# Eight PSUM banks dealt out anew: three for the scores, two for the row maxima

## What is computed

```python
x = x + 0.5 * ffn(layernorm(x), ...)        # 8 experts, top 2 for each row, a gate at the end
x = x + attention(layernorm(x), ...)        # 16 heads of 8 columns, causal, a linear bias by distance
x = x + 0.5 * ffn(layernorm(x), ...)

# attention, for each of 8 batch entries:
att = einsum("bhqd,bhkd->bhqk", q, k) / sqrt(8) + alibi      # 16 heads, 512 queries, 512 keys
att = softmax(where(causal, att, -inf), axis=-1)
y = einsum("bhqk,bhkd->bhqd", att, v)
out = y @ o_w + o_b
```

## Time and profile before

| | |
|---|---|
| time, median of 3 runs | 887.24 us (885.19 to 888.77) |
| profiled execution, its own time | 885.58 us |
| its span in the profile | 883.8 us |
| mean granted TensorE clock | 0.913 of full speed |
| TensorE matmul busy | 683.1 us (77%) |
| VectorE, ScalarE, GpSimd busy | 568.2, 410.8, 485.6 us |

### The profile page before, as it was taken

The page is one execution under the profiler, slowest core; times in us unless marked ns, Lnnn a source line. Parts: engine busy times, 40 slices in busy tenths (PEclk is TensorE's granted clock), DMA queues, the critical chain, the costliest instruction groups (busy, mean ns, idle before and its releaser), DMA issues.

```text
span 883.8 us, 16149 instructions
## 1 busy us (share of the span) xinstructions
PE 683.1 (77%) x4719; PEld 492.3 (56%) x4719; DVE 568.2 (64%) x1922; ACT 410.8 (46%) x931; POOL 485.6 (55%) x588
## 2 busy tenths in 40 slices
PE   1465667979897798997988979999997777838760
PEld 1355656979793354654646545455544466837750
DVE  3675545968767876876767767787673235745538
ACT  2243411545560265664545645556554655615530
POOL 2656554034512666576866768373645466566661
PEclk9968777988898899998999999999997999969985
DMA  8614544744348313023050240302201235233525
GB/s 242 205 48 117 132 123 115 183 112 105 94 113 192 110 31 98 18 65 87 2 130 21 49 103 1 98 17 55 61 13 53 85 78 167 75 93 84 175 96 154
DMA packets 89825, 84.04 MB, mean 95 GB/s; under 512 B 14561, under 2 KB 72556, under 8 KB 89580
## 3 DMA queue, kind: packets, MB, share of 16 engines
q1 hardware_dynamic: 74472, 57.51, 25.8%
q0 software_dynamic: 8800, 19.72, 7.5%
q10 hardware_dynamic: 6468, 5.79, 2.8%
HBM read 43.84 MB, written 31.13 MB: 85 GB/s over the span
## 4 chain that ended last, share of the span: by engine, by line
PE 46%; DVE 15%; another core or an unknown queue 11%; issue 7%; ACT 7%; SPq 5%; ACTq 3%; DMA 3%; POOL 1%; DVEq 0%; POOLq 0%
PE bank L2361 6%; PE bank L2271 6%; PE bank L2401 6%; PE bank L2286 6%; PE bank L2426 6%; SPq L595 4%; DVE mx_of L1923 3%; PE pair L2449 2%; PE bank L2363 2%; ACT beside_parts L1254 2%; DMA qT<-mT_zero 2%; PE pair L2213 2%; PE bank L2246 1%; ACT arena L1326 1%
## 5 line engine op out<-in xcount | busy, mean ns | idle before, releaser
L1326 ACT ACTIVATE arena<-bank 128x512 f32<-128x512 f32 x320 | 184.0, 599 | 175.2 <-PE bank L2401 147.1
L1923 DVE TENSOR_REDUCE mx_of<-bank 128x4 f32<-128x512 f32 x320 | 204.2, 684 | 81.9 <-PE bank L2361 42.9
L2401 PE MATMUL bank<-qT,kZ 128*128 128x512 f32 (+3 forms) x512 | 156.9, 377 | 19.2 <-ACT arena L1326 12.4
L975 POOL TENSOR_SCALAR_AFFINE_SELECT arena<-arena 128x256 f32<-128x256 f32 (+1 forms) x192 | 95.4, 521 | 123.9 <-ACT arena L1326 122.5
L2361 PE MATMUL bank<-kZ,qT 128*128 128x512 f32 x320 | 148.5, 481 | 15.7 <-DVE mx_of L1923 6.2
L2401 PEld LDWEIGHTS bank<-qT,kZ 128*128 128x128 f32 x512 | 95.7, 197 | 49.2 <-ACT arena L1326 24.1
L868 POOL DMA_INDIRECT z_rows<-beside_kZ,place x80 | 78.7, 984 | 51.5 <-DVE place L1685 29.8
L2361 PEld LDWEIGHTS bank<-kZ,qT 128*128 128x128 f32 x320 | 63.1, 200 | 70.7 <-issue 31.4
L885 POOL DMA_INDIRECT sums<-y_rows,y_place x56 | 54.4, 971 | 84.9 <-DMA y_rows<-arena 70.0
L2426 PE MATMUL bank<-arena,vA 128*9 128x512 f32 (+3 forms) x1024 | 92.4, 440 | 5.2 <-POOL arena L975 2.7
L1254 ACT ACTIVATE beside_parts<-bank,hidden_bias 128x128 f32<-128x128 f32 x160 | 45.5, 381 | 69.6 <-remote 44.0
(11 more groups left out here) (286 smaller groups left out, 1306.7 us busy)
## 6 DMA issues: line engine op xcount, KB each, us to landing
arena<-z_rows SPq DMA_DIRECT2D x128, 66.0 KB
qT<-parts SPq DMA_DIRECT2D x42, 128.0 KB
kZ<-parts SPq DMA_DIRECT2D x168, 32.0 KB
y_rows<-arena SPq DMA_DIRECT2D x20, 264.0 KB, 3.3
kZ<-bias_k_r SPq DMA_DIRECT2D x8, 512.0 KB
beside_kZ<-y_rows SPq DMA_DIRECT2D x7, 528.0 KB, 3.9
z_rows<-in_spare SPq DMA_DIRECT2D x4, 528.0 KB
z_rows<-in_spare SPq DMA_DIRECT2D x32, 66.0 KB
```

Source lines behind the costliest of these rows:

```text
L975: g_.affine_select(out=cut, in_=cut, compare_op=ALU.is_ge, fill=0.0, base=0, pattern=[[0, 2], [0, blocks], [1, P]], channel_multiplier=-1) ...
L1326: a_(dst, src, ACT.Exp).then_inc(exp_ok.sem, 1)
L1923: v.tensor_reduce(mx_of[:, queries, :, t, keys], ps_a[n % NA][:, :].rearrange("p (q n) -> p q n", q=NQ), AX.X, ALU.max).then_inc(reduced.s ...
L2401: return mm(outp, kZ[u][:, h, lo:lo + P], qT[u][:, t, lo:SEQ], start=start, stop=True, skip_group_check=(kind != "full"))
```

## The change

Bank 4 goes from the maximum units to the score units. `ps_a` has two banks (0, 1): maximum unit n waits for the reduction of unit n - 2. `ps_b` has three (2, 3, 4): score unit n waits for the exponential of unit n - 3. Since 40 is no multiple of three, the score ring doesn't start anew with each batch but runs on over its end: unit n of batch b is in bank (40 b + n) mod 3. The last batch has a ring of five (2, 3, 4, 0, 1), entered where the other one stopped; its first five units wait for all exponentials of the batch before and for all reductions. Three waits at the seam to the second experts are worked out anew from the banks (in the diff in this order: the first transposes into banks 2 and 3, the first `up` into 0 and 1, the first `down` into bank 4), and batch 0's first score units wait for `y_weighted` too, since bank 4 was one of the experts'.

```diff
-        ps_a, ps_b, ps_o, ps_m = [banks[0], banks[1], banks[4]], banks[2:4], banks[5], banks[6:8]
+        ps_a, ps_b, ps_o, ps_m = banks[0:2], banks[2:5], banks[5], banks[6:8]
         NA = len(ps_a)
-        ps_b_last = ps_b + ps_a[:2]
+        ps_b_last = ps_b + ps_a
+        last_first = N_UNITS * (BATCH - 1) % len(ps_b)
 
         def score_bank(b, n):
-            ring = ps_b_last if isinstance(b, int) and b == BATCH - 1 else ps_b
-            return ring[n % len(ring)], len(ring)
+            if b == BATCH - 1:
+                return ps_b_last[(n + last_first) % len(ps_b_last)], len(ps_b_last)
+            return ps_b[(N_UNITS * b + n) % len(ps_b)], len(ps_b)
+
+        def last_unit_in(bank_):
+            return max(n for n in range(N_UNITS) if score_bank(BATCH - 1, n)[0] is bank_)
...
-                        wait(pe, exp_ok, BATCH - 1, N_UNITS - 3 + q)
+                        wait(pe, exp_ok, BATCH - 1, 1 + last_unit_in(ps_x[q % 2]))
...
-                        wait(pe, exp_ok, BATCH - 1, N_UNITS - 1 + p)
+                        wait(pe, exp_ok, BATCH - 1, 1 + last_unit_in(ps_up[p % 2]))
...
-                        wait(pe, reduced, BATCH - 1)
+                        wait(pe, exp_ok, BATCH - 1)
...
                 if early(b, 0) and n < ring:
                     wait(pe, x_out, 0)
-                elif ring == 2:
-                    pe.wait_ge(exp_ok.sem, exp_ok.value(b, n - 1))
-                elif n < 2:
-                    wait(pe, exp_ok, b - 1)
+                    wait(pe, y_weighted, 0)
+                elif b < BATCH - 1:
+                    pe.wait_ge(exp_ok.sem, exp_ok.value(b, n - ring + 1))
                 elif n < ring:
+                    wait(pe, exp_ok, b - 1)
                     wait(pe, reduced, b)
                 else:
                     wait(pe, exp_ok, b, n - ring + 1)
```

More of the change, by code:

```diff
@@ L2388, in scores @@
                     wait(pe, x_out, 0)
-                elif ring == 2:
-                    pe.wait_ge(exp_ok.sem, exp_ok.value(b, n - 1))
-                elif n < 2:
+                    wait(pe, y_weighted, 0)
+                elif b < BATCH - 1:
+                    pe.wait_ge(exp_ok.sem, exp_ok.value(b, n - ring + 1))
+                elif n < ring:
                     wait(pe, exp_ok, b - 1)
-                elif n < ring:
                     wait(pe, reduced, b)
```

## The result

| | before | after |
|---|---|---|
| median of 4 runs each | 888.0 us (885.19 to 892.74) | 907.4 us (903.75 to 910.38) |
| profiled execution, span | 885.58, 883.8 us | 903.75, 901.9 us |
| mean granted TensorE clock | 0.913 | 0.907 |

The account below looks back on a forecast made before the run. TensorE was taken to bound batches 0 to 6, VectorE the maxima of batch 0. 16 (maximum bank) + 3 (maxima) - 2 (score bank) + 0.5 (seam) = +17.5 us on 885.58, as a median 905 us, range 888 to 922.

Parts of the forecast that it names:

- third maximum bank: Batches 0 to 6: its loss makes TensorE wait for later reductions, 2.3 us a batch, +16 us (+7 to +39).
- third score bank: Waits of score units for exponentials: only short ones, mostly in batch 0, go; -2 us (0 to -12.4).
- A: Slot 0, four maximum units in a row: unit 3 waits for the second reduction, not the first; +0.6 us a batch.
- maxima of batch 0: Stretch led by VectorE: two-bank loop slower, first half hidden by a DMA wait, second not; +3 us (1 to 5).
- C: Slot 11, two maximum units in a row: the second waits +0.8 us, half counted before the first `values`; +0.4 a batch.
- D: Slots 20 to 22, reductions run after layer norm statistics: units 26 and 27 wait one reduction longer; +0.65 us a batch.
- E: Slot 28, run of five reductions: maximum unit 33 waits longer; +0.35 us a batch.
- F: Slot 33: unit 39 waits +0.6 us longer, of which the DMA behind the maxima leaves +0.3 a batch.
- absorbed: Rival: each delay falls into TensorE's existing idle time, no change, median 890 us; chance 0.08.
- B: Slot 5, maximum unit 8 waits over a microsecond longer, but the score unit behind could go earlier; 0.
- The third score bank wins: Rival: long stops of batches 2 to 4 come from the two-bank score ring and vanish, median 880 us; chance 0.10.
- The clock: Rival: new short waits give each batch another half-clock spell, 2.75 us each, 19 in all, about 924 us; chance 0.10.

Follow-up runs that it names:

- e1: Kernel before with two maximum banks instead of three, score ring still two, bank 4 unused in the attention: 893.3 us, ratio 1.011 to the kernel before.
- e3: Changed kernel, but its score ring of three starts anew with each batch: 895.71 us, ratio 1.0153 to the kernel before.
- e5: Changed kernel run again, unaltered, on another chip: 900.5 us, ratio 1.0214 to the kernel before.
- e7: Changed kernel with maximum reductions that read only half of the columns: 888.64 us, ratio 1.0067 to the kernel before.
- e9: Kernel before with the four indirect DMAs for the second half of z moved later on GpSimd's list: 894.67 us, ratio 1.0058.
- e11: Two maximum and two score banks, bank 4 unused, with the same DMA move as e9: 907.24 us, ratio 1.0218 to the kernel before.
- e10: Changed kernel with the same DMA move as e9: 911.33 us, ratio 1.0249 to the kernel before.
- e12: Kernel before with first-half z DMAs moved behind the next batch's first zeroing, second-half ones behind its third: 900.86 us, ratio 1.0124.
- e4: Changed kernel, with the last batch's ring entered so that its last exponential is in bank 4: 895.18 us, ratio 1.015 to the kernel before.
- e2: Kernel before with bank 4 added to the score ring of the last batch alone: 883.1 us, ratio 1.0011.
- e8: Kernel before with four maximum banks and a single score bank, last batch as before: 941.11 us, ratio 1.0685.

## Why the prediction was right

The direction and the cause of the loss were right: losing the third maximum bank costs, and a third score bank does not pay for it. The sum came out close partly by luck, for some of its terms were wrong in opposite directions. The third score bank was forecast some 8 us too low; site A was forecast 4 us too high, the maxima of batch 0 by 3 in this pair of profiles.

**The third maximum bank: right in kind, and at three sites in size.** Over seven batches C was forecast at +2.8 us and is +2.2, D +4.6 and is +5.4, E +2.5 and is +2.5 (first table). All three are there in e1, e3 and e5 as well. VectorE's full ring holds TensorE, and TensorE's other work behind the maximum unit is late with it. That the length of a reduction sets the loss is shown for E (e7); for C and D it is read from the waits.

**F: right in size; A: wrong.** Forecast +2.1 and +4.2 us. F takes 3.6 us in slot 32, and 2.1 of them come back in slot 36, where before TensorE waited for VectorE's maxima (7.7 us for seven slots before, 5.6 after, 5.6 in e1). So 1.5 stay. A part of the delay is hidden, as forecast, but by that wait and not by the DMA behind it. A lies in slot 39, which takes 22.2 us for 22.5. Two of the seven are long in the profile before (batches 0 and 3, 5.2 and 4.6 us, with waits for loads of operands as well), and executions differ there: 19.4 in e9, which has the banks of before, 19.1 in e1. So A costs nothing that can be told from this spread. In its place TensorE waited less for the DMA of the maxima (late weight loads 4.3 us instead of 6.7 over the same stretch). This is the *absorbed* rival's mechanism, at A and at half of F.

**B: right with two score banks, wrong with three.** e1 has 0 in slots 0 to 8, as priced. The change itself has +6.5.

**The third score bank: wrong, -2 forecast.** It costs 6.7 us in the batches (e1 against after) and 5.0 (e11 against e10). The step rightly held that the long stops would not go; that short waits for exponentials would turn into 2 us of gain was wrong. They went (21.6 us of late weight loads to 9.1 in e1 and 3.9 with the bank), and no time went with them. One gain of the forecast size is there: slot 38 takes 2.7 us over the seven batches with three score banks and 4.9 with two (e1). The slot behind gives it back (22.2 for 19.1; 21.4 in e5), in part in waits for the DMA of the maxima. What e12 adds is that the stop has its cause outside both rings. *Why* the third bank makes slots 0 to 8 longer is settled for a part only. With it, TensorE comes to slot 4 of batches 5 and 6 early and stands there for a reduction (1.75 and 1.61 us; 1.26 and none over 1 in e1), and a spell at half clock follows. Slots 5 to 8 of these two batches then take 9.7 us, in all four executions with whole reductions and the ring running on (after, e4, e5, e10), and 6.9 with two score banks (e1, e11). The ring started anew (e3) has these stops but not the spells, and also 6.8. That is 2.8 us of the 6.5. The rest is spread over the other batches and isn't explained; the long stops begin earlier in batches 2 and 3 and end as late (4.6 and 4.5 us for 4.05 and 4.19). Batch 0's 2.3 us more in slots 0 to 4 are there with two score banks too. Whether the bank would be worth something without the stop was not tried.

**Maxima of batch 0: the loop right, the 0 in part luck.** Forecast +3, measured 0. The two-bank loop is slower, and by more than forecast (0.73 us a unit for 0.68). The whole of the first half's delay went into the DMA wait of 2.99 us, as forecast. The second half's reductions took 14.5 us (285.66 to 300.14) for 12.8 (283.91 to 296.70), 1.7 more, though the kernel before was at half clock for 5.4 us of it and the changed one never. With three banks and no half clock (e12) they took 12.1, so the loop itself costs some 2.4. The steps behind the reductions then took 6.2 us for 7.5, up to the first score unit: VectorE's part of them 1.0 us for 2.7 (296.73 to 299.39 before, 300.17 to 301.18 after), where before they ran beside GpSimd's tensor operations. Neither the clock nor the place of GpSimd's operations is the change's. With three maximum banks the stretch took 32.7 to 35.5 us (before, e2, e9, e12), with two 34.9 to 35.5 in the five executions with 6 us or less at half clock. These two have the least half clock of each group (e12, then e3):

```profile
269.31:302.00 32.69, 24.38 (x66) 10.43 (x66) 29.00 (x48) 2.17 (x3) 14.16 (x16) 0.90 0.60 161
265.24:300.22 34.98, 24.69 (x67) 10.06 (x67) 29.76 (x48) 2.17 (x3) 16.92 (x19) 1.00 0.59 156
```

In e1, at half clock for nearly all of it, the same stretch cost 6.7 us, beyond the 1 to 5, and in e10, with 21 us at half clock, it took 39.4: what the loop costs hangs on the clock that it meets.

**The seam: right in kind.** Forecast +0.5 out of 0 to 0.9, measured 1.0, just above its end (e4 takes it back).

The sum in the profiled execution: 15.8 in the batches, 0.0 for the maxima and 1.0 at the seam are the change's, 16.8 of 17.5 forecast. The rest of the difference (2.0 us in the first experts, -3.7 in batch 7, 2.8 in the second experts) is not put down to the change: the first experts are untouched by it, and over the fourteen profiles the second experts take 172.5 to 180.1 us, 172.5 to 175.6 where TensorE was at half clock for under 50 us of them and 175.0 to 180.1 where for over 50. Batch 7 has 10 us at half clock in the profile before and 3 after, and is 38.6 us in e1 and 39.7 in e9, which has the banks of before; but the other kernels with three maximum banks have 41.1 (e2, e12), so a part of it may be the change's after all. Between sets there is a spread that stays unexplained: 1.0199 and 1.0214 for the change, 1.015 for e4, which differs by the seam's 1 us.

**The rivals.** *Absorbed* held at A and for half of F. *The third score bank wins* fell with e1, and so did its premise with e12. *The clock*: TensorE was at half clock for 25 us of batches 0 to 6 instead of 17, in pieces of 3.4 us, most of them in slots 4 to 9 at or behind the stop. One lies in batch 5 (587.00 below) and one in batch 6, where before there was none. They make the clock of these batches 0.969 and 0.967 (1.00 before), just under the 0.97 that the prediction named as a sign of being wrong. So this rival is true in small: 2.8 us in slots 5 to 8, of the 19 it was priced at. The Trainium skill, page "TensorE: Matmul & The Clock Gate", section "A second HAM failure mode: psum-queue depth-cycling", tells of a kernel whose clock swung between its levels from such short waits. Of the new short waits, the trace agrees for two, 1.75 and 1.61 us in slot 4 of batches 5 and 6, behind which the clock fell. Behind one of 1.55 us in slot 20 of batch 6 it didn't. From 604.00 to 622.00, sites D and E, where reductions hold TensorE for up to 0.75 us, it was 1.00:

```profile
587.00:590.40 3.40, 3.40 (x15) 2.97 (x12) 2.33 (x5) 1.79 (x3) 2.84 (x5) 0.50 0.16 44
...
604.00:622.00 18.00, 16.73 (x104) 10.19 (x103) 13.11 (x28) 11.43 (x22) 8.18 (x12) 1.00 0.07 15
```

**What should have shown it.** Idle for reductions above 15 us: 32.7, or 21.5 without the long stops. Late weight loads in more than 60 pieces: 85. Late loads for exponentials down to a few: 6. Batches of 375 to 380 us, spread evenly: 378.5; single batches lose 0.7 to 3.7 us. The 19 reductions taking 14 to 16 us: 13.7, under it. No batch without a stop under a clock of 0.97: batches 5 and 6 fell just under it.

## What to carry to other kernels

With a ring, ask first which consumer comes in runs behind other work: it needs the depth, the one that takes its results one by one needed two banks here and no more (e8: 62 us for the second; e1 and e11: 5 to 7 us lost by the third). Price a lost bank site by site as the time of one reduction more where the ring was full, then look where the next wait of the same engine is for something slow (here VectorE's maxima and their DMA), for what is taken just ahead of it can be free. A stop at which several engines are released together by nothing that the profile names was not the ring's here: look at what another engine issues during it, and move that.

## What the runs showed of the hardware

A stop of TensorE, VectorE and ScalarE together, up to 4.7 us of TensorE's time (e10), while GpSimd issues four indirect DMAs in a row (1.0 us each, 0.3 apart) behind two gathers and SyncE its loads: with these four moved (e12) the stop was gone, and rows of four in other places (e9, e12) made none of this kind. A row of gathers in batch 0 of e12 made one of 4.0 us. Whether it is the DMA traffic or the way of the signals that is slow then stays open. The Trainium skill, page "Perfetto Trace Analysis", section "DMA Instruction — SWDGE (GPSIMD)", says that the profile ends such an instruction when its descriptors are written, not when the data have moved. No run here shows when these data had moved; the engines were let go at 473.3, 1.6 us after the last of the four had ended by the profile (471.7).

A reduction of 512 columns takes 0.68 to 0.69 us, and one that is issued right behind another begins 0.60 us after it (five in 3.08 us before). Two in a row do so with a ring of two as well (1.29 us), but a run of five takes 3.39, since the later ones must wait for their units.

Small operations of VectorE were stretched beside GpSimd's tensor operations, and those that were ended 0.05 to 0.08 us after GpSimd's had ended. In the kernel before, two took 0.78 us (to 297.97, GpSimd's to 297.91) and 1.29 us (to 299.39, GpSimd's to 299.31), and in the changed one without them 0.20 and 0.22. In e5, the same changed kernel, one took 0.78 (to 297.02, GpSimd's to 296.97), so it is a matter of how the two engines fall together. Not every small operation there is stretched: a copy that began 0.01 us after GpSimd's operation took 0.20.
